# A pairwise-interaction kernel: K and Q loaded together with half pieces of F, TensorE's filling from the first tile on, and a first row block of the last tile spread over four banks

## The reference

```
Kf  = einsum('bjd,ed->bje', F, K_w)
S   = einsum('bid,bjd->bij', F, Kf)
out = einsum('bij,ijd->bid', S, W)
out = out + einsum('bid,ed->bie', F, Q_w)
```

## Time and profile before

| | us |
|---|---|
| median of 3 runs | 607.75 (607.74 to 608.13) |
| the profiled execution's own time | 608.0 |
| its span, from the first to the last instruction | 606.2 |
| PE busy | 597.5 (99% of the span) |
| PEld busy | 527.0 (87%) |
| ACT busy | 401.5 (66%) |
| DVE busy | 398.7 (66%) |

### The profile page before, as it was taken

The page is one execution under the profiler, slowest core; times in us unless marked ns, Lnnn a source line. Parts: engine busy times, 40 slices in busy tenths (PEclk is TensorE's granted clock), DMA queues, the critical chain, the costliest instruction groups (busy, mean ns, idle before and its releaser), DMA issues.

```text
span 606.2 us, 17908 instructions
## 1 busy us (share of the span) xinstructions
PE 597.5 (99%) x7693; PEld 527.0 (87%) x7693; DVE 398.7 (66%) x412; ACT 401.5 (66%) x698; POOL 0.2 (0%) x4
## 2 busy tenths in 40 slices
PE   9999999999999999999999999999999999999995
PEld 7888989889898898988889898898988989889894
DVE  6556757567685665947659475686756768567376
ACT  7978393874938659295692947839387493865830
POOL 0000000000000000000000000000000000000000
PEclk9999999999999999999999999999999999999998
DMA  8543847548575575755647566385755757457177
GB/s 324 239 141 145 322 169 282 199 177 312 189 281 173 212 262 208 280 200 208 246 183 284 204 248 241 140 322 173 285 197 186 304 196 282 173 211 259 66 279 278
DMA packets 29452, 137.60 MB, mean 227 GB/s; under 512 B 3264, under 2 KB 4032, under 8 KB 21312
## 3 DMA queue, kind: packets, MB, share of 16 engines
q1 hardware_dynamic: 20592, 75.38, 31.5%
q10 hardware_dynamic: 8784, 61.08, 28.4%
HBM read 69.34 MB, written 67.11 MB: 225 GB/s over the span
## 4 chain that ended last, share of the span: by engine, by line
PE 98%; DVE 1%; issue 1%; DVEq 0%
PE ps L501 20%; PE ps L440 20%; PE ps L442 19%; PE ps L441 19%; PE ps L527 18%; DVE o_sb L371 1%; PE ps L557 1%; DVEq L46 0%; PE ps L457 0%; PE ps L461 0%; PE ps L459 0%; DVE o_sb L380 0%; DVE f_hi L385 0%
## 5 line engine op out<-in xcount | busy, mean ns | idle before, releaser
L336 DVE TENSOR_TENSOR f_lo<-f_ring,f_hi 128x1024 fp32r<-128x1024 f32 x124 | 151.8, 1224 | 169.6 <-ACT f_hi L214 167.9
L228 ACT ACTIVATE q_out<-ps 128x512 f32<-128x512 f32 x256 | 156.9, 613 | 6.4
L219 ACT ACTIVATE kf<-ps 128x512 f32<-128x512 f32 x256 | 155.9, 609 | 3.4
L371 DVE TENSOR_TENSOR o_sb<-ps,q_out 128x1024 f32<-128x1024 f32 x127 | 145.1, 1213 | 19.3 <-PE ps L527 19.3
L237 ACT ACTIVATE s_t<-ps 128x512 f32<-128x512 f32 x32 | 19.1, 598 | 176.5 <-PE ps L501 176.5
L501 PE MATMUL ps<-f_ring,kf 128*64 128x64 f32 x4096 | 124.1, 222 | 0.4 <-issue 0.4
L501 PEld LDWEIGHTS ps<-f_ring,kf 128*64 128x64 f32 x4096 | 121.6, 138 | 2.9 <-issue 0.8
L527 PEld LDWEIGHTS ps<-s_t,w_sb 64*128 64x128 f32 x2048 | 115.6, 188 | 5.6 <-issue 5.6
L527 PE MATMUL ps<-s_t,w_sb 64*128 64x128 f32 x2048 | 118.6, 274 | 0.0
L440 PE MATMUL ps<-f_hi,k_hi 128*128 128x512 f32 x254 | 100.7, 397 | 0.0
L440 PE MATMUL ps<-f_hi,q_hi 128*128 128x512 f32 x256 | 99.9, 390 | 0.0
(11 more groups left out here) (36 smaller groups left out, 164.3 us busy)
## 6 DMA issues: line engine op xcount, KB each, us to landing
out<-o_sb SPq DMA_DIRECT2D x127, 512.0 KB, 3.5
f_ring<-f_t ACTq DMA_DIRECT2D x58, 1024.0 KB, 4.8
f_ring<-f_t SPq DMA_DIRECT2D x4, 1024.0 KB, 10.4
w_sb<-w SPq DMA_DIRECT2D x1, 2048.0 KB, 18.8
f_ring<-f SPq DMA_DIRECT2D x6, 256.0 KB, 5.1
out<-o_sb SPq DMA_DIRECT2D x2, 256.0 KB, 2.4
f_ring<-f SPq DMA_DIRECT2D x3, 128.0 KB, 2.6
f_ring<-f ACTq DMA_DIRECT2D x1, 128.0 KB, 4.3
```

Of the source, the lines that this page charges most:

```text
L219: nc.scalar.activation(kf[:, c // 2, c % 2 * CK:(c % 2 + 1) * CK, :, :].rearrange("d k h i -> d (k h i)"), ps[:, 2 * c % 8, :], COPY).then ...
L228: nc.scalar.activation(q_out[:, t % 2, :, :].rearrange("d i (h b) -> d i h b", h=2)[:, :, :, at:at + CK], q_bank(t * CHUNKS + c).rearrange ...
L336: nc.vector.tensor_tensor(f_lo[:, v % SPLIT, :], f_unit(v), f_hi[:, v % SPLIT, :].bitcast(F32), ALU.subtract).then_inc(flo_done, 1)
L371: nc.vector.tensor_tensor(o_sb[:, n % OBUF, :, :], ps[:, bank:bank + 2, :], q_out[:, t % 2, :, :].rearrange("d (s m) b -> d s (m b)", s=2) ...
```

## The change

K transposed and the first 256 columns of F's piece 0 stand side by side in one array of the input, Q transposed and the other 256 columns in a second (`first`, each 128 x 384). Each is one load, the first on SP's queue and the second on ScalarE's, into a slot of `o_sb`. Piece 1 comes whole on SP and piece 2 whole on ScalarE's queue, then 3 to 7, then piece 0 once more into `f_ring`, from which the scores read it; scores of unit 0 wait for it. Only chunk 0 has its K product made in halves, with hi x lo ahead of lo x hi. VectorE makes the high and the low part of the first half, ScalarE the high part of the second. `WARM` is 6.

The filling is 368 waits in chunks 8 to 15 of tile 0 (184 wait instructions), 108 in tiles 1 to 14 (before: none in tiles 0 and 1, 58 in tile 2), 130 in tile 15.

In the last tile the first row block goes into four banks, two for its first two rows and two for the last two, and each half sum takes two rows of both halves of the features: the first can begin after half of the block's matmuls (`o_half`). Its stores are cut in the same way. The banks of the other blocks, and what they wait for, follow from that.

```diff
-WARM = 7
+WARM = 6
-FILL = {2: 58}
-FILL.update((t, 108) for t in range(3, TILES - 1))
-FILL[TILES - 1] = 132
+FILL = {0: 368}
+FILL.update((t, 108) for t in range(1, TILES - 1))
+FILL[TILES - 1] = 130
...
+        raw = o_sb[:, 0, :, :].rearrange("d s n -> d (s n)")
+        first_cols = [slice(h * FC, (h + 1) * FC) for h in range(2)]
+        k_raw, q_raw = raw[:, 0:D], raw[:, FC:FC + D]
+        f_raw = [raw[:, h * FC + D:(h + 1) * FC] for h in range(2)]
...
+        def row_bank(t, k):
+            return [0, 6, 4, 0, 2, 6, 4, 0][k] if t == TILES - 1 else 2 * k % 8
...
-            load_half(0)
-            load_half(1)
-            load_half(3)
-            for c in range(2, PIECES):
+            sp.dma_start(raw[:, first_cols[0]], first[0, :, :]).then_inc(first_in[0], 16)
+            load_first(1)
+            for c in range(3, PIECES):
                 load_first(c)
+            load_first(0)
...
+            rows_0 = out[t, 0, :, :].rearrange("d (s n) -> d s n", s=2)
             sp.wait_ge(out_half, 1)
-            sp.dma_start(out[t, 0, :, 0:IR * P], o_sb[:, slot, 0, :]).then_inc(o_stored[slot], 16)
+            sp.dma_start(rows_0[:, :, half_cols(0)], o_sb[:, slot, :, half_cols(0)]).then_inc(o_stored[slot], 16)
             sp.wait_ge(out_done, t * UNITS + 1)
-            sp.dma_start(out[t, 0, :, IR * P:2 * IR * P], o_sb[:, slot, 1, :]).then_inc(o_stored[slot], 16)
+            sp.dma_start(rows_0[:, :, half_cols(1)], o_sb[:, slot, :, half_cols(1)]).then_inc(o_stored[slot], 16)
...
-            act.dma_start(k_raw, k_t).then_inc(k_in, 16)
-            act.dma_start(q_raw, q_t).then_inc(q_in, 16)
-            act.dma_start(f_half_cols(2), f_0[1, :, half_cols(0)]).then_inc(f_half[2], 16)
-            act.wait_ge(k_in, 16)
+            act.dma_start(raw[:, first_cols[1]], first[1, :, :]).then_inc(first_in[1], 16)
+            act.dma_start(f_cols(2), f_0[2, :, :]).then_inc(f_first[2], 16)
+            act.wait_ge(first_in[0], 16)
             nc.scalar.activation(k_hi[:, :], k_raw, COPY).then_inc(khi_done, 1)
-            split_half(0)
-            split_half(1)
-            act.wait_ge(q_in, 16)
+            act.wait_ge(first_in[1], 16)
+            nc.scalar.activation(f_hi[:, 0, half_cols(1)], f_raw[1], COPY).then_inc(fhi_first, 1)
             nc.scalar.activation(q_hi[:, :], q_raw, COPY).then_inc(qhi_done, 1)
-            split_half(2)
-            split_half(3)
+            split_first(1)
...
-            def half_sum(k, half):
+            def half_sum(half):
+                t = TILES - 1
+                m = half * (IR // 2)
                 return nc.vector.tensor_tensor(
-                    o_sb[:, n % OBUF, half, :], ps[:, bank + half, :],
+                    o_sb[:, t * UNITS % OBUF, :, half_cols(half)], ps[:, 2 * half:2 * half + 2, 0:BANK // 2],
+                    q_out[:, t % 2, :, :].rearrange("d (s m) b -> d s (m b)", s=2)[:, :, m * P:(m + IR // 2) * P],
                     ALU.add)
...
+            dve.wait_ge(first_in[0], 16)
+            nc.vector.tensor_copy(f_hi[:, 0, half_cols(0)], f_raw[0]).then_inc(fhi_dve, 1)
+            dve.wait_ge(fhi_dve, 1)
+            low_half(0)
             dve.wait_ge(khi_done, 1)
...
-            low_half(0)
+            dve.wait_ge(fhi_first, 1)
             low_half(1)
...
-            dve.wait_ge(o_done, n + 1)
+            dve.wait_ge(o_half, 1)
             dve.wait_ge(q_copied, TILES * CHUNKS)
...
-            half_sum(0, 0).then_inc(out_half, 1)
-            half_sum(0, 1).then_inc(out_done, 1)
+            half_sum(0).then_inc(out_half, 1)
+            dve.wait_ge(o_done, n + 1)
+            half_sum(1).then_inc(out_done, 1)
...
-                    for x in range(FILL.get(t, 0) * c // CHUNKS, FILL.get(t, 0) * (c + 1) // CHUNKS):
-                        pe.wait_ge(zeros_done, 1)
+                    if t >= 1 or c >= 8:
+                        a, b = (c - 8, CHUNKS - 8) if t == 0 else (c, CHUNKS)
+                        for x in range(FILL[t] * a // b, FILL[t] * (a + 1) // b):
+                            pe.wait_ge(zeros_done, 1)
...
+                        if e == 0:
+                            pe.wait_ge(f_first[0], 16)
...
+                    at, col = (bank + 2 * (x // 2), x % 2 * P) if split else (bank, x * P)
...
+                    if split and x == IR // 2 - 1:
+                        ins.then_inc(o_half, 1)
...
-                    if k >= 4:
+                    if t == TILES - 1 and k >= 3:
+                        pe.wait_ge(out_half if k == 3 else out_done, 1 if k == 3 else t * UNITS + k - 3)
+                    elif k >= 4:
```

More of the change, by code:

```diff
@@ L32, with build @@
 OBUF = 5
-WARM = 7
+WARM = 6
 LATE = 2
-FILL = {2: 58}
-FILL.update((t, 108) for t in range(3, TILES - 1))
-FILL[TILES - 1] = 132
+FILL = {0: 368}
+FILL.update((t, 108) for t in range(1, TILES - 1))
+FILL[TILES - 1] = 130
 BOTH = [v for v in range(FIRST, TILES * UNITS) if v in (4, 5) or v >= UNITS and v % UNITS in (0, 4, 6)]
-def build(nc, f_0, f_t, k_t, q_t, w, out):
+def build(nc, first, f_0, f_t, w, out):
     with ExitStack() as ctx:
@@ L80, in build @@
         ps = psum("ps", [P, 8, BANK])
-        f_half = [sem(f"f_half{n}") for n in range(4)]
+        first_in = [sem(f"first_in{n}") for n in range(2)]
         f_first = [sem(f"f_first{n}") for n in range(PIECES)]
         f_in = [sem(f"f_in{n}") for n in range(RING)]
-        k_in, q_in, w_in = sem("k_in"), sem("q_in"), sem("w_in")
+        w_in = sem("w_in")
         o_stored = [sem(f"o_stored{n}") for n in range(OBUF)]
@@ L95, in build @@
         s_done, s_copied, s_copied_act = sem("s_done"), sem("s_copied"), sem("s_copied_act")
-        o_done, out_done, out_half = sem("o_done"), sem("out_done"), sem("out_half")
+        o_done, out_done = sem("o_done"), sem("out_done")
+        o_half, out_half = sem("o_half"), sem("out_half")
+        def row_bank(t, k):
+            return [0, 6, 4, 0, 2, 6, 4, 0][k] if t == TILES - 1 else 2 * k % 8
         def q_bank(c):
@@ L309, in low_half @@
             def low_half(h):
-                dve.wait_ge(fhi_first, h + 1)
-                nc.vector.tensor_tensor(f_lo[:, 0, half_cols(h)], f_half_cols(h), f_hi[:, 0, half_cols(h)].bitcast(F32),
+                nc.vector.tensor_tensor(f_lo[:, 0, half_cols(h)], f_raw[h], f_hi[:, 0, half_cols(h)].bitcast(F32),
                                         ALU.subtract).then_inc(flo_first, 1)
@@ L350, in both_f @@
                 nc.vector.tensor_copy(f_hi[:, v % SPLIT, :], f_unit(v)).then_inc(fhi_dve, 1)
-                dve.wait_ge(fhi_dve, 3 + sum(1 for x in BOTH if x <= v))
+                dve.wait_ge(fhi_dve, 4 + sum(1 for x in BOTH if x <= v))
                 low_unit(v)
@@ L450, in q_product, with k_halves @@
                       f_lo[:, c // 2 % SPLIT, piece_cols(c)]).then_inc(q_done, 1)
[L452 to L456, removed]
+            def k_halves():
+                pe.wait_ge(khi_done, 1)
+                for h in range(2):
+                    dst, cols = ps[:, 0, half_cols(h)], half_cols(h)
+                    pe.wait_ge(fhi_first if h else fhi_dve, 1)
                     nc.tensor.matmul(dst, k_hi[:, :], f_hi[:, 0, cols], start=True, stop=False)
+                    pe.wait_ge(flo_first, h + 1)
+                    nc.tensor.matmul(dst, k_hi[:, :], f_lo[:, 0, cols], start=False, stop=False)
                     pe.wait_ge(klo_done, 1)
-                    nc.tensor.matmul(dst, k_lo[:, :], f_hi[:, 0, cols], start=False, stop=False)
-                    pe.wait_ge(flo_first, h + 1)
-                    ins = nc.tensor.matmul(dst, k_hi[:, :], f_lo[:, 0, cols], start=False, stop=True)
+                    ins = nc.tensor.matmul(dst, k_lo[:, :], f_hi[:, 0, cols], start=False, stop=True)
                 ins.then_inc(k_done, 1)
@@ L467, in project @@
                     n = t * CHUNKS + c
[L468 to L471, removed]
+                    if n == 0:
+                        k_halves()
+                        pe.wait_ge(qlo_done, 1)
                         q_product(n)
@@ L518, in row_block @@
             def row_block(t, k):
-                bank = 2 * k % 8
+                bank = row_bank(t, k)
+                split = t == TILES - 1 and k == 0
                 for x in range(IR):
                     m = k * IR + x
+                    at, col = (bank + 2 * (x // 2), x % 2 * P) if split else (bank, x * P)
                     for s in range(2):
@@ L526, in row_block @@
                             cols = cols[:, ::-1, :]
-                        ins = nc.tensor.matmul(ps[:, bank + s, x * P:(x + 1) * P], w_sb[half, m, :], cols,
+                        ins = nc.tensor.matmul(ps[:, at + s, col:col + P], w_sb[half, m, :], cols,
                                                start=True, stop=True)
+                    if split and x == IR // 2 - 1:
+                        ins.then_inc(o_half, 1)
                 ins.then_inc(o_done, 1)
@@ L571 @@
     f = np.asarray(r_F).reshape(B // (2 * UB), 2 * TOK, D)
```

(3 more changed lines are left out.)

25 lines of the change are left out of this document (6 added, 19 removed).

## The result

The changed kernel takes 615.06 us (median of 4, 614.92 to 616.13) against 607.75 (606.76 to 608.13): ratio 1.0127, 95% interval 1.0109 to 1.0144. It is 7.3 us slower; the forecast was 606.8. The profiled execution took 616.13 us, with a span of 614.3 against 606.2.

A forecast was written before the change was run, and what follows sets the result against it. TensorE work was taken to bound 98% of the span, VectorE the tail. Head 0.5, filling 0.2 and tail 0.3 us sum to 1.0 us, so 606.8 us from the median of 607.75; range 605.7 to 608.1.

The forecast's parts named there:

- the price of a wait instruction: Tile 0, chunks 8 to 15: 15 ns per wait, taken from the scores, bounds 15 and 350 ns, so hidden behind TensorE.
- the 74 ns from which the rival decided: Tile 0's filling costs more than it hides above 74 ns a wait; at 100 ns 611.6 us; chance 0.12.
- the 4.1 us taken: Tile 0, chunks 8 to 15: the sequencer's lead over TensorE, up to three chunks, 4.1 us.
- The filling's other half: All tiles: added waits shift where 256-instruction blocks end, removing some stalls; gain 0.2 us, ends 1.3 and -0.4.
- their 0.16 us: Projections of tile 2: the excess from a stall at a block's end would go, 0.16 us.
- the state of the transfers: Scores of tiles 1, 2 and 15: it decides whether a stall comes, so only 0.05 us was taken, for tile 1.
- the blocks realigned heal the scores too: Scores of tiles 1, 2 and 15: stalls go or halve, 0.9 us more gained, 605.9 us; chance 0.22.
- The head: Start of the kernel: new first loads land in 2.75 us, chunk 2 starts at 7.8 in place of 8.27; gain 0.5 us.
- where 5.0 was taken: Start: piece 1, now a second issue on SP at about 1.15 us, lands at 5.0 us; 5.7 if late.
- the thin transfers after 3.4 us: Start: transfers at 109 GB/s between 3.42 and 4.40 us, against 342 later, spoke for piece 1 landing late.
- The slow pace: Start: a 0.15 us gap after the filler products may delay TensorE's faster pace; priced at nothing, 0.2 us at worst.
- The tail: Last tile: first half sum 0.46 us earlier, but the next sum waits for row block 1; 0.3 us kept.

The follow-up runs named there:

- x2: Changed kernel with half the filling in tile 0 (184 waits in place of 368): 614.40 us, ratio 1.0104.
- x3: Changed kernel with one and a half times the filling in tile 0 (552 waits): 635.76 us, one run.
- x1: Changed kernel without the filling in tile 0, all else as changed: 614.88 us, ratio 1.010.
- z1: Changed kernel with eight filler products and the filling spread (216 waits over chunks 4 to 15 of tile 0, 238 in tile 1): 615.33 us, ratio 1.0120.
- w2: Kernel before with the new tail and spread filling, as y4 but 234 waits in tile 1 in place of 238: 618.39 us, ratio 1.0157.
- z2: Kernel before with no filling in any tile: 616.03 us, ratio 1.0141.
- y2: Changed kernel with the kernel before's filling, so new head and tail only: 607.88 us, ratio 0.9994.
- y1: Kernel before with the new tail alone: 607.90 us, ratio 1.0002.
- y4: Kernel before with the new tail and the filling spread (216 waits over chunks 4 to 15 of tile 0, 238 in tile 1): 607.13 us, ratio 0.9984.
- y3: Changed kernel with the kernel before's filling and eight filler products in place of six: 606.88 us, ratio 0.9983.
- z3: Kernel before with six filler products in place of seven: 607.73 us, ratio 0.9994.
- w3: As z1, but 240 waits in tile 1 in place of 238: 606.51 us in one run.

## Why the prediction was wrong

**The step that failed: the price of a wait instruction.** "I take the row of 15 ns, the same sequencer" was the step. It costs 109 ns (x2, x3), seven times as much, and above the 74 ns from which the rival decided. The row of the scores has no wait instructions in it, and nothing says that a wait passes at the pace of a matmul. "Their own price stands in no row" is true of the rows chosen, not of the trace: the kernel before has 496 of the filling's wait instructions in it (L490), and where two wait instructions stand side by side they start 0.106 us apart (median of 295 pairs). The bounds were 15 and 350 ns, the rival's point lay well inside, and 0.12 was too low a chance for it. At 109 ns the rival's own formula gives 184 x 0.109 + 1.4 - 15.1 = 6.4 us in tile 0; the kernel lost 8.0 in tile 0, mainly because the lead was smaller than the 4.1 us taken. From chunk 8's start at 17.74 to the scores at 36.89 are 19.15 us, against 8 x 2.6 = 20.8 of sequencer time: a lead of 1.7 us.

**The filling's other half: block ends right, gain too small.** The place of the block ends was read rightly from two stalls, and x1, x2, z1 and w2 have theirs at the counted place within one or two instructions. Tile 2's projections lost their 0.16 us as forecast. But the changed kernel is clean in all tiles 1 to 14, 1.05 us where 0.2 were forecast: the stalls of tiles 1 and 2, which I had put down to the state of the transfers, went, and with them those of tiles 5 and 9, which the prediction doesn't name. This is the rival "the blocks realigned heal the scores too", all but tile 15, whose stall stayed. The transfers do have a part in it, as the packets above show, but the shift (by three instructions in tile 2 and later) was enough to change it. And I saw only the shift's small gain, not what not shifting costs: with the filling of tiles 1 to 14 in place, tile 0's can't be left out (x1, 614.88). So the changed kernel pays 8.0 us in tile 0 for what is otherwise 6.6 us of stalls in tiles 1 to 14: two losses of about one size, and x1 merely swaps them. The section "Instruction fetch mechanics" of the Trainium skill's page "Runtime: NRT & Kernel Launch" holds the crossing of a block to be mostly hidden. The 16 KB agree here (64 packets, 1.05 MB). "Mostly hidden" agrees in the rows and nearly everywhere in the projections; in the scores it doesn't, and z2 is 8 us over the kernel before.

**The head: two terms mis-sized, one of them by chance.** The 192 KB loads landed in 3.3 and 3.4 us, not 2.75. Piece 1 landed 4.0 us after its issue at 1.18, at 5.2 where 5.0 was taken, and the thin transfers after 3.4 us were not there (399 GB/s from 3.3 to 4.5 us). The slow pace, priced at 0.2 us at worst, lasted till 9.05 in this execution, which makes +1.28 of the forecast -0.5. It did so in x1 too (8.96), but ended at 7.0 in x2 and x3 and at 5.2 in y2, all with the same head: that is the part of chance. With the old filling y2 leaves room for a head that costs some 0.7 us, so its share of the 7.3 us is not settled by the medians; the profiled execution was the slowest of four, by 1.0 us.

**The tail: right up to the sums.** Half sums at 0.80 us (0.75 forecast), the wait for row block 1, whole sums 0.31 earlier. The last store's landing took part of it back: 0.17 at the end of the span where 0.3 were forecast.

What stays open: why the instruction block's packet mostly starts 1.4 us into the scores at places 31 to 41, and 2.4 or 3.1 us into them at 43, and what in the data transfers, if they are the cause, decides it. When the slow pace ends differs from execution to execution with the same head (y1, y4 at about 7 us, z2 and the kernel before at about 5.6). With eight filler products it ended by 6.3 us in all four traces; more than that y3 and z3 don't settle.

## What to carry to other kernels

A wait that has long been met is not free on TensorE: 0.109 us of sequencer time, so a run of them is hidden only up to the queue's work beside it; divide the stage's time per group by that price before placing them. In a long unrolled stream any edit that adds or removes an instruction moves all block ends behind it; count them modulo 256 against the densest stage, and compare kernels only at equal places, or the shift (8.8 us from z1 to w3, and 11.3 from w2 to y4, for two instructions, between medians of different chips) is taken for the edit's own effect. Look in the trace for the instruction blocks' own packets: a stall of this kind follows a packet that started late.

## What the runs showed of the hardware that was not expected

- A wait instruction of two met waits took 0.109 us of TensorE's sequencer, 0.106 from start to start in the traces; the scores' instructions took 0.015 each.
- Place of a block's end in stages of 512 instructions at 15 ns, tiles 2 to 14: clean or nearly so at 31, 36, 37, 38, 40 and 41; at 34, stalls in three of the kernel before's thirteen tiles; at 43, stalls in every tile, mean period 37.6 (z1) and 37.9 (w2); at 129, 201 and 221, stalls in all but one, 37.4 to 37.6.
- After each of the 104 stalls in the scores TensorE went on 1.2 to 1.6 us after the 16 KB packet of its instruction block had ended; in tile 0's scores, with the DMA engines all but idle, no trace has a stall at any place.
- Two concurrent first loads of 192 KB landed in 2.9 to 3.4 us over the executions, where those of 64 KB and 128 KB issued at the same time took 2.2 to 2.8.
- With products 0.43 us apart up to 9 us into the program, the granted clock of the profile read 1.00 in every stretch of the start.
